# Row-axis position terms copied once per quarter over all partitions and moved by DMA

## What is computed

```python
attn = jnp.einsum('bqd,bkd->bqk', q * SCALE, k)
r_q = q.reshape(b * NH, h, w, HD)
rel_h = jnp.einsum('bhwc,hkc->bhwk', r_q, Rh)
rel_w = jnp.einsum('bhwc,wkc->bhwk', r_q, Rw)
attn = attn.reshape(b * NH, h, w, h, w) + rel_h[:, :, :, :, None] + rel_w[:, :, :, None, :]
attn = jax.nn.softmax(attn.reshape(b * NH, hw, hw), axis=-1)
out = jnp.einsum('bqk,bkd->bqd', attn, v)
```

## Time and profile before

| | us |
|---|---|
| median of 3 runs | 2853.99 |
| lowest and highest | 2850.5, 2854.19 |
| profiled execution, its time | 2852.06 |
| its span | 2849.7 |
| mean granted TensorE clock | 0.981 |

### The profile page before, as it was taken

How to read it: one execution, slowest core, us unless ns; L and a number is a source line. 1 busy time by engine, 2 the same in 40 slices (tenths; PEclk the granted TensorE clock), 3 DMA queues, 4 the chain that set the end, 5 groups by cost and what they waited for, 6 DMA issues and landing times.

```text
span 2849.7 us, 69244 instructions
## 1 busy us (share of the span) xinstructions
PE 2638.5 (93%) x29116; PEld 1547.0 (54%) x29116; DVE 1973.6 (69%) x3617; ACT 2058.2 (72%) x2450; POOL 1763.1 (62%) x1195
## 2 busy tenths in 40 slices
PE   7899998999999999999989999899998999989995
PEld 4465644656456564565635656365554655546562
DVE  8775767666775767757677576775767758677574
ACT  6686866859668586785777767778767777678683
POOL 5474775737667375673766746666575665757473
PEclk8899999999999999999999999999999999999998
DMA  3100011000100001000020000200002000010000
GB/s 117 32 2 1 2 35 46 2 1 2 57 24 2 1 2 57 23 2 1 2 66 14 2 1 6 75 2 2 1 9 72 2 2 1 12 46 2 1 2 23
DMA packets 36116, 53.66 MB, mean 19 GB/s; under 512 B 5824, under 2 KB 32704, under 8 KB 35808
## 3 DMA queue, kind: packets, MB, share of 16 engines
q1 hardware_dynamic: 34304, 48.64, 5.5%
q10 hardware_dynamic: 1504, 0.61, 0.1%
HBM read 30.95 MB, written 12.58 MB: 15 GB/s over the span
## 4 chain that ended last, share of the span: by engine, by line
PE 51%; POOL 16%; ACT 12%; issue 11%; DVE 10%; DMA 0%; POOLq 0%; ACTq 0%; DVEq 0%; SPq 0%
POOL pl L1049 15%; PE ps L556 12%; PE ps L932 7%; PE ps L851 5%; PE ps L889 4%; PE ps L902 4%; PE ps L713 4%; ACT p L983 4%; PE ps L1140 4%; DVE qb L701 3%; PE ps L891 3%; ACT ph L963 3%; PE ps L1339 2%; ACT p L1351 2%; PE ps L1359 2%
## 5 line engine op out<-in xcount | busy, mean ns | idle before, releaser
L1049 POOL TENSOR_TENSOR pl<-p,ph 128x1024 f16<-128x1024 f32 (+2 forms) x672 | 1095.2, 1642 | 378.4 <-ACT ph L963 372.6
L1007 DVE TENSOR_REDUCE mxp<-ps 128x1 f32<-128x512 f32 (+2 forms) x1344 | 784.0, 626 | 258.8 <-PE ps L851 253.0
L983 ACT ACTIVATE p<-ps 128x1024 f32<-128x1024 f32 (+1 forms) x672 | 641.0, 954 | 175.8 <-PE ps L902 175.0
L963 ACT ACTIVATE ph<-p 128x1024 f16<-128x1024 f32 (+1 forms) x672 | 669.3, 996 | 21.9
L932 PEld LDWEIGHTS ps<-v,ph 128*128 128x128 f16 x9600 | 506.2, 97 | 128.4 <-issue 27.7
L932 PE MATMUL ps<-v,ph 128*128 128x65 f16 (+1 forms) x9600 | 531.0, 194 | 17.2 <-POOL pl L1049 16.7
L932 PE MATMUL ps<-v,pl 128*128 128x65 f16 x4800 | 509.1, 192 | 0.0
L932 PEld LDWEIGHTS ps<-v,pl 128*128 128x128 f16 x4800 | 446.7, 99 | 0.0
L902 PE MATMUL ps<-qc,kc 65*128 65x512 f16 (+3 forms) x1344 | 380.0, 364 | 0.0
L1049 DVE TENSOR_TENSOR pl<-p,ph 128x512 f16<-128x512 f32 (+1 forms) x336 | 243.8, 726 | 184.4 <-ACT ph L963 183.4
L730 POOL TENSOR_TENSOR v<-o,v 128x384 f16<-128x384 f32 x128 | 116.1, 918 | 369.3 <-ACT o L726 368.7
(11 more groups left out here) (190 smaller groups left out, 5077.7 us busy)
## 6 DMA issues: line engine op xcount, KB each, us to landing
xin<-in_x SPq DMA_DIRECT2D x8, 1536.0 KB, 7.0
x<-in_x SPq DMA_DIRECT2D x8, 1536.0 KB, 7.0
out<-x SPq DMA_DIRECT2D x16, 768.0 KB, 4.4
qc<-qa SPq DMA_DIRECT2D x42, 128.0 KB, 2.3
p<-in_L_conv_qkv_w SPq DMA_DIRECT2D x3, 576.0 KB, 10.2
qc<-rowt SPq DMA_DIRECT2D x96, 2.0 KB
x<-in_L_attn_Wq SPq DMA_DIRECT2D x1, 576.0 KB, 8.1
x<-in_L_attn_Wk SPq DMA_DIRECT2D x1, 576.0 KB, 9.3
```

The lines of the kernel that those rows point to most:

```text
L963: self.nc.scalar.activation(m.ph[:, i % RING, :, 0:w], m.p32[:, i % RING, :, 0:w], ACT.Copy).then_inc(self.s["hi"], 1)
L983: nc.scalar.activation(m.p32[:, i % RING, :, 0:w], m.ps[:, 2 * (i % 2):2 * (i % 2) + 2, 0:w], ACT.Exp, scale=SCALE).then_inc(s["exp"], 1)
L1007: nc.vector.reduce_max(m.mxp[:, h % 2, kh, qt:qt + 1], m.ps[:, bank, 0:w], AX.X).then_inc(s["free"], 1)
L1049: engine.tensor_tensor(m.pl[:, i % RING, part, 0:w], m.p32[:, i % RING, part, 0:w], m.ph[:, i % RING, part, 0:w], ALU.subtract).then_inc(s ...
```

## The change

From the second image on (`before` is set), the row axis goes another way. One ScalarE instruction per quarter copies all 128 partitions of PSUM, in the row axis's order of values, as float16 into a buffer in the first three ring buffers of `p32` (`rel_held`); one VectorE instruction does the low part likewise. Of the four parts in it, the two of the row axis are moved by DMA to the same partitions of `qa` or `qb` (32 partitions x 3 heads x 256 values, 48 KB, pieces of 512 bytes): two DMAs per quarter and part, 16 an image. The column axis keeps its two instructions per quarter and engine.

New waits: ScalarE's copy of quarter 0 waits for `each` = 5 (the gelu outputs in the buffers that it overwrites were read); VectorE's first subtraction waits for all three copies of its quarter; TensorE's first score product waits for all high moves, and the first attention product for all low ones. The moves stand in SP's queue around the second store.

```diff
+    def rel_quarter_high(self, act, n):
+        act.wait_ge(self.s["rel_mm"], self.s.at("rel_mm", n + 1))
+        held = self.rel_held(n, 0).rearrange("p (s i w) -> p s i w", s=NPAIR, i=8)
+        self.nc.scalar.activation(held, self.rel_rows(n), ACT.Copy).then_inc(rel["rows_hi"], 1)
+        for parity in range(2):
+            src, dst = self.rel_views(4 * n + 2 * parity + 1, self.m.qa)
+            self.nc.scalar.activation(dst, src, ACT.Copy).then_inc(rel["columns_hi"], 1)
+    def rel_rows_low(self, dve, n):
+        dve.wait_ge(rel["columns_hi"], rel.at("columns_hi", 2 * n + 2))
+        self.nc.vector.tensor_tensor(lo, self.rel_rows(n), hi, ALU.subtract).then_inc(rel["rows_lo"], 1)
+    def rel_rows_move(self, sp, n, part):
+        sp.wait_ge(rel[ready], rel.at(ready, n + 1))
+        for parity in range(2):
+            b = self.rel_base(parity, 0)
+            sp.dma_start(buf[b:b + IMG, parity * NPAIR:(parity + 1) * NPAIR, 8 * IMG * n:8 * IMG * (n + 1)],
+                         self.rel_held(n, part)[b:b + IMG, :].rearrange("p (s q) -> p s q", s=NPAIR)).then_inc(rel[("moved_hi", "moved_lo")[part]], 16)
+    def rel_lows_ready(self, pe, quarters):
+            pe.wait_ge(self.rel["columns_lo"], self.rel.at("columns_lo", 2 * quarters))
+        if self.rel and quarters == 4:
+            pe.wait_ge(self.rel["moved_lo"], self.rel.at("moved_lo", 128))
+    def rel_highs_ready(self, pe):
+            pe.wait_ge(self.rel["columns_hi"], self.rel.at("columns_hi", 8))
+            pe.wait_ge(self.rel["moved_hi"], self.rel.at("moved_hi", 128))
...
-            pe.wait_ge(qkv0.s["rel_hi"], qkv0.s.at("rel_hi", RELS))
-            pe.wait_ge(qkv0.s["rel_lo"], qkv0.s.at("rel_lo", RELS - 4))
+            qkv0.rel_highs_ready(pe)
+            qkv0.rel_lows_ready(pe, 3)
...
             if w.next:
-                for r in range(4):
-                    w.next.qkv0.rel_high(act, r)
+                act.wait_ge(ff.s["each"], ff.s.at("each", ff.PAIRS - 1))
+                w.next.qkv0.rel_quarter_high(act, 0)
...
-            w.ff.store(sp, out_tiles[b], stored)
+            w.ff.store(sp, 0, out_tiles[b], stored)
+            if w.next:
+                for n, part in ((0, 0), (0, 1), (1, 0), (1, 1), (2, 0)):
+                    w.next.qkv0.rel_rows_move(sp, n, part)
+            w.ff.store(sp, 1, out_tiles[b], stored)
+            if w.next:
+                for n, part in ((2, 1), (3, 0), (3, 1)):
+                    w.next.qkv0.rel_rows_move(sp, n, part)
```

More of the change, by code:

```diff
@@ L529, in __init__ @@
         self.late = None
+        self.rel = None
     def high(self, k, t0, t1):
@@ L701, in rel_low, with rel_held, rel_rows @@
         self.nc.vector.tensor_tensor(lo, src, hi, ALU.subtract).then_inc(self.s["rel_lo"], 1)
+    def rel_held(self, n, part):
+        return self.m.p32[:, 0:RING - 1, :, :].rearrange("p r a b -> p (r a b)").bitcast(F16)[:, (2 * n + part) * 8 * NPAIR * IMG:(2 * n + part + 1) * 8 * NPAIR * IMG]
+    def rel_rows(self, n):
+        return self.rel_out(n).rearrange("p i (s w) -> p s i w", s=NPAIR)
+    def rel_quarter_high(self, act, n):
+        rel = self.rel
+        act.wait_ge(self.s["rel_mm"], self.s.at("rel_mm", n + 1))
[4 more added lines that the diff above has]
+            self.nc.scalar.activation(dst, src, ACT.Copy).then_inc(rel["columns_hi"], 1)
@@ new lines, in rel_rows_low, with rel_columns_low @@
+    def rel_rows_low(self, dve, n):
+        rel = self.rel
+        dve.wait_ge(rel["columns_hi"], rel.at("columns_hi", 2 * n + 2))
+        hi, lo = (self.rel_held(n, part).rearrange("p (s i w) -> p s i w", s=NPAIR, i=8) for part in range(2))
+        self.nc.vector.tensor_tensor(lo, self.rel_rows(n), hi, ALU.subtract).then_inc(rel["rows_lo"], 1)
+    def rel_columns_low(self, dve, n):
+        for parity in range(2):
+            src, hi = self.rel_views(4 * n + 2 * parity + 1, self.m.qa)
+            _, lo = self.rel_views(4 * n + 2 * parity + 1, self.m.qb)
+            self.nc.vector.tensor_tensor(lo, src, hi, ALU.subtract).then_inc(self.rel["columns_lo"], 1)
@@ new lines, in rel_rows_move @@
+    def rel_rows_move(self, sp, n, part):
+        rel, buf = self.rel, (self.m.qa, self.m.qb)[part]
+        ready = ("rows_hi", "rows_lo")[part]
+        sp.wait_ge(rel[ready], rel.at(ready, n + 1))
+        for parity in range(2):
+            b = self.rel_base(parity, 0)
+            sp.dma_start(buf[b:b + IMG, parity * NPAIR:(parity + 1) * NPAIR, 8 * IMG * n:8 * IMG * (n + 1)],
+                         self.rel_held(n, part)[b:b + IMG, :].rearrange("p (s q) -> p s q", s=NPAIR)).then_inc(rel[("moved_hi", "moved_lo")[part]], 16)
@@ new lines, in rel_lows_ready @@
+    def rel_lows_ready(self, pe, quarters):
+        if self.rel:
+            pe.wait_ge(self.rel["columns_lo"], self.rel.at("columns_lo", 2 * quarters))
+        else:
+            pe.wait_ge(self.s["rel_lo"], self.s.at("rel_lo", 4 * quarters))
+        if self.rel and quarters == 4:
+            pe.wait_ge(self.rel["moved_lo"], self.rel.at("moved_lo", 128))
+    def rel_highs_ready(self, pe):
+        if self.rel:
+            pe.wait_ge(self.rel["columns_hi"], self.rel.at("columns_hi", 8))
+            pe.wait_ge(self.rel["moved_hi"], self.rel.at("moved_hi", 128))
+        else:
+            pe.wait_ge(self.s["rel_hi"], self.s.at("rel_hi", 16))
@@ L1394, in add, with store @@
         self.nc.gpsimd.tensor_tensor(x, self.widened(n).rearrange("p t a b -> p t (a b)"), x, ALU.add).then_inc(self.s["added"], 2)
-    def store(self, sp, out_ap, stored):
-        for hf in range(2):
-            t = slice(4 * hf, 4 * hf + 4)
-            sp.wait_ge(self.s["added"], self.s.at("added", 4 * (hf + 1)))
-            sp.dma_start(out_ap[:, t, :], self.m.x[:, t, :]).then_inc(stored, 16)
+    def store(self, sp, hf, out_ap, stored):
+        t = slice(4 * hf, 4 * hf + 4)
+        sp.wait_ge(self.s["added"], self.s.at("added", 4 * (hf + 1)))
+        sp.dma_start(out_ap[:, t, :], self.m.x[:, t, :]).then_inc(stored, 16)
 class Dram:
@@ L1559, in scalar @@
                 for n in w.with_v[t]:
+                    if before:
+                        qkv0.rel_quarter_high(act, n)
+                        continue
                     for r in range(4 * n, 4 * n + 4):
@@ L1585, in scalar @@
             if w.next:
-                for r in range(4):
-                    w.next.qkv0.rel_high(act, r)
+                act.wait_ge(ff.s["each"], ff.s.at("each", ff.PAIRS - 1))
+                w.next.qkv0.rel_quarter_high(act, 0)
         def vector(dve, w, before):
             qkv0, attn0, proj0, ln, qkv1, attn1, ff = w.qkv0, w.attn0, w.proj0, w.ln, w.qkv1, w.attn1, w.ff
-            for r in range(4 if before else 0, RELS - 2):
-                qkv0.rel_low(dve, r)
+            for r in range(RELS - 2):
+                if not before:
+                    qkv0.rel_low(dve, r)
+            for n in (1, 2, 3):
+                if before:
+                    qkv0.rel_rows_low(dve, n)
+                if before and n < 3:
+                    qkv0.rel_columns_low(dve, n)
             for u in attn0.prologue:
@@ L1597, in after_row @@
                 for r in range(RELS - 2, RELS):
-                    qkv0.rel_low(dve, r)
+                    if not before:
+                        qkv0.rel_low(dve, r)
+                if before:
+                    qkv0.rel_columns_low(dve, 3)
             attn0.vector(dve, after_row)
@@ L1622, in vector @@
             if w.next:
-                w.next.qkv0.rel_low(dve, 0)
+                w.next.qkv0.rel_rows_low(dve, 0)
             ff.widen(dve, 2)
@@ L1626, in vector @@
             if w.next:
-                for r in range(1, 4):
-                    w.next.qkv0.rel_low(dve, r)
+                w.next.qkv0.rel_columns_low(dve, 0)
         def gpsimd(pool, w, before):
```

6 lines of the change are left out of this document (4 added, 2 removed).

## The result

| | before | after |
|---|---|---|
| median us | 2851.86 | 2861.82 |
| lowest, highest | 2848.73, 2867.58 | 2852.41, 2867.53 |
| runs | 20 | 20 |
| profiled execution: time, span | 2852.06, 2849.7 | 2862.61, 2860.9 |
| its mean granted clock | 0.981 | 0.978 |

What follows compares the result with a forecast made beforehand. VectorE's subtractions were taken to bound the seven passages between images; five gaining 1.2 us and two 2.8 made 11.6 off the profiled 2852.06, giving 2840.5, plus 1.9 for the median: 2842.4 us, range 2828 to 2855.

Steps and rivals of the forecast that it cites:

- What bounds the kernel: Between images, VectorE sets the passage's end twice: subtraction 12 holds TensorE until 780.18, subtraction 14 holds the maxima until 782.04.
- The copies: 128-partition row copies replace two per quarter on each engine: 0.82 us on ScalarE, 0.95 on VectorE in the profile.
- rival 4: A 128-partition copy takes longer than one of 32, say 1.6 us on ScalarE: 2860 us, chance 0.04.
- ScalarE: Between images, a new 0.6 us wait for down products; last column copy done at 776.3, 2.4 us earlier than before.
- VectorE: Before the maxima, 10 subtractions instead of 14, nine of them in a row from 769.23; VectorE free at 778.1.
- The moves: SP's queue between images: issues of 0.55 us each, last high move landing at 779.1, which releases TensorE's first score product.
- rival 1: Moves behind the store: 512-byte packets cost as much as 2 KB ones, last high move lands at 782.0; 2867 us.
- the likeliest case: Moves land near 779 between images, clock falls in some passages only: 2834 to 2849 us, chance 0.58.
- The sum: TensorE starts scores 1.1 us earlier; five passages gain 1.2 us and two gain 2.8, 11.6 us in all.
- rival 2: Between images, moves land between 779.7 and 780.6, a DMA wait replacing VectorE's: 2850 to 2857 us, chance 0.16.
- The price of the fall: At TensorE's score start, a passage gains 1.2 us if the clock falls, 2.8 if it stays up.
- a possible gain at 739: The clock's fall at 739 might come in some images only, worth 1 to 1.5 us an image; no gain counted.

Runs made afterwards that it cites:

- highs_first: Changed kernel with the high moves of quarters 2 and 3 issued ahead of low ones, second store before only the last low move: 2828.54 us, 0.9916 of before.
- store_last: Changed kernel with only the second store moved, behind all moves: median 2847.18 us, 0.9989 of before.
- no_moves: Changed kernel without the sixteen moves per image and without TensorE's waits for them: 2828.43 us, 0.9922 of before.
- the two profiles: The changed kernel's first profiled execution, 2862.61 us, and one from rerunning it unchanged, 2855.18 us (rerun median 2863.20, 1.0038 of before).
- one_more: Kernel before plus one unused VectorE maximum of 0.9 us in each image after the first: 2862.00 us, 1.0033 of before.

## Why the prediction was wrong, point by point

**What bounds the kernel: right.** VectorE's subtractions set the end of the passage twice, and freed of them (highs_first) TensorE begins at 777.33 and the maxima at 778.02, as worked out.

**The copies: right to 0.01 us.** 0.812 and 0.958 us against 0.82 and 0.95; time goes by columns, so rival 4 fell.

**ScalarE: right.** Quarter 0 ends at 764.29 + 1.63 = 765.92 (765.9 forecast), the last column copy at 776.32 (776.3). Its new wait for the down products:

```profile
  PE ps L1413: 4.7, 7
```

4.7 us in seven images are 0.67 each, against 0.6.

**VectorE: right.** Nine in a row, free at 778.14 (778.1).

**The moves: the step that failed.** The prediction had TensorE released by the last high move at 779.1; it was released by it at 780.2, which is all of the 1.1 us that the passage was to gain. The order of the queue was right; the issue times in it were too small. From the end of quarter 1's row subtraction to the last high issue I had 4.6 us; it was 778.08 - 772.23 = 5.85. Term by term: an issue takes 0.62 us, not 0.55 (four ahead of the store and one of quarter 3: 0.35 us); the store's takes 0.59, not 0.39 (0.2); the pair behind the store 1.97, not 1.10 (0.9); and the 0.3 us that SP should have waited for low of quarter 2 took some of it up. With the few hundredths between issues that is 1.25 us. I had a row of 0.63 (L1099) beside it and took 0.55, and had no row for an issue close behind a store. (My expectations for highs_first and store_last speak of 1.37 us for the first issue behind a store; it is the second, 1.33 to 1.35, in all passages but the last.) Landing was shorter than the median of its queue, 2.1 us and not 2.3. So 779.1 became 780.2. The price of packets, over which rival 1 turned, did not matter: no_moves and highs_first are alike, and the last high move, behind the store, landed in 2.1 us, where the least of any move is 2.0. Store_last is the check of the other terms: with TensorE at 779.15 its passages gain 13.6 us in the profile, against 11.6, and its median of 2847.18 lies in the 2834 to 2849 of the likeliest case. The Trainium skill (DMA: Bandwidth & Descriptors, Rules for kernel authors) has the rule that transfers under 64 KB pay mostly overhead. No run here joins the moves, so its advice is not tried; but these of 48 KB did cost mostly something else than their bytes, 2.0 us at the least to land, and besides 0.6 us of issue each, 16 an image, one behind the other on SP. The estimate of the same page for one transfer, 2.1 us (Anatomy of one DMA; it is given there for transfers that GpSimd issues, and these are issued by SP), lies between the 2.0 at the least and the 2.3 in the median; the longest took 3.7.

**The sum.** 780.2 is inside rival 2, *nothing won*, with a landing between 779.7 and 780.6, to which I gave 0.16. In the passages it came as that rival said: +2.8 and +1.4 us over seven in the two profiles, against the 11.6 that the forecast took off. What a start is worth without a fall of the clock was worked out rightly: by the same steps (twelve maxima back to back behind the later of VectorE and TensorE) highs_first should have its thirteenth at 778.1 + 8.1 + 0.1 = 786.3, and has it at 786.2. The price of the fall was 2.8 - 1.2 = 1.6 us in the forecast and is 1.7 in store_last, where it comes in four passages of seven, against five of seven. Only the start was never that early in the kernel of the change. In spans the forecast was 2838.1 and the profile 2860.9: of these 22.8 us, 14.4 are the passages (from 11.6 won to 2.8 lost), and 8.4 are the next point.

**What no case had: the loss elsewhere.** "First image and last tail don't change", I wrote, and put nothing on the clock beyond the passage, except a possible gain at 739. Rival 2 ended at 2857; the median is 2861.8. In the first profile this was 8.4 us, in the second 2.4. One_more shows that such a loss needs nothing of the change: a single operation of 0.9 us per image brings one too. What is shown is that the sites of the falls differ, that time goes with the mean clock, and that two kinds of operation of VectorE meet GpSimd's at a shift of 0.1 to 0.2 us. That the change's own loss outside the passages is nothing but such a shift is likely by this, not shown. What stays open is why before has its falls at the same two places in every image from image 1 to the seventh's end (739 and 780, and every 348.15 us after), and other phases have more of them, and how much of the 3 to 6 us at the same mean clock is the image-1 stall (2.0 by its rows) and how much small waits in the passages. A version with that stall taken out was not tried.

## What to carry to other kernels

When work is moved from an engine to DMAs, write the issuing queue down as an engine of its own, with the issue time of each transfer and the readiness of each, and put those first whose reader comes first: here the order alone was worth 33 us, and turned 10 us lost into 25 won. An in-order queue makes a transfer that nobody needs yet, but that is not ready, a wait for all behind it. And a forecast of some tenths of a per cent in a program with a clock that moves needs a term for phase; a run with an unrelated small delay is a cheap way to size it.

## What the runs showed of the hardware

- One SP issue of a move of 32 partitions x 3 x 512 bytes takes 0.60 us in the median. 15 of 112 took over 1 us, up to 1.39; in six of seven passages one of them is the second issue behind the second 768 KB store. With that store behind all moves (store_last) 7 did. One store's issue takes 0.38, or 0.59 right behind other issues. Landing is 2.0 us at the least, 2.3 in the median, 3.7 at the most in the kernel of the change.
- An operation of VectorE with two inputs in SBUF that starts behind one of GpSimd waits until that ends: 2.62 us for 0.69 (0.05 and 0.06 us behind), 2.04 and 2.00 for 0.17 (0.11 and 0.14 behind). Their ends fit: 796.22 and half of 4.31 is 798.37, and 796.36 + 2.00 is 798.36. Where VectorE starts first, by 0.04 to 0.13 us, it takes its usual time, and GpSimd's takes 2.54 instead of 2.13 in the pair of image 1. The Trainium skill (SBUF — State Buffer, Who interferes with whom) says of the pair of SBUF ports that VectorE and GpSimd share that it is an exclusive lock, held for the whole instruction by whichever starts first; the rows agree in who waits, and with the ends within 0.2 us (a VectorE operation that began only at GpSimd's end would be done 0.17 us later than 798.36 is, and 0.14 later than 511.18).
- At the same gap of 2.07 us ahead of the scores, the granted clock fell in some passages of one execution and not in others (store_last), and a fall there cost 1.7 us; one in the feed-forward at 739 cost 1.1 (highs_first, no_moves).
- The mean granted clock of the kernel of the change lies between 0.975 and 0.982 from run to run, and 0.001 of it goes with some 2.1 us of 2860.
